# Gate and up products of the shared FFN in two fp16 parts

## The chip, the cores and the metric

The kernel is one program on one core of a Trainium2 chip. The metric is the device time of an execution in microseconds (us). It computes an adaLN transformer block: attention with 16 heads over two sequences of 2048 tokens of width 256, then a feed-forward part (FFN) made of a shared expert that sees every token and eight routed experts, one for each token.

## The reference, cut to what matters

```python
h = layernorm(x) * (1 + ca) + sa
x = x + ga * attention(h)                      # 16 heads of 16, LoRA folded into the weights
h = layernorm(x) * (1 + cb) + sb               # called h2 in the kernel
logits = h @ gate_w.T                          # 4096 x 8
top_id, score = argmax(logits), sigmoid(max(logits))
shared = (silu(h @ shared_gate.T) * (h @ shared_up.T)) @ shared_down.T     # F = 512
routed = swiglu of expert top_id on h * score
x = x + gb * (shared + routed)
```

All of it is in f32 at the outside; 4096 tokens, width D = 256 (two halves of 128), F = 512 (four blocks of 128).

## The kernel before, in words

Tokens go in eight chunks of 512. The kernel has no scheduler: every engine has a stream written out by hand, and semaphores join them.

**Heads** (attend_tensor, attend_vector, attend_scalar, attend_gpsimd, attend_sync). For each of 32 heads TensorE makes score products twice: once for the row maxima, into a ring of three PSUM banks that VectorE reduces (L1374; one in eight is folded in with ScalarE's help, L1416, L1371), and once for the exponentials, which ScalarE takes (L1437) and TensorE multiplies with the values (L1305). The maxima are made one to two heads ahead. These score products are in fp16 parts already (L1237, L1293). ScalarE copies the finished head out of PSUM (L1443). SP's stream has a list of transfers by head, in `prepare(n)`: with head 9 it loads `wuT` and `wdT`, the shared FFN's weights. GpSimd's stream has elementwise work of other stages by head (bias of the residual rows with heads 4 and 7, for example), each time ahead of `split_maxima`, whose `mb` the head's scores need. In head 20 VectorE inverts the first sums in eight pieces (L1071).

**Merge** (merge_tensor, merge_vector, merge_scalar, merge_sync). For each chunk: output projection (L1652), residual (L1721) and moments on VectorE, root (L1757), VectorE's factors, normalisation on ScalarE (L1764, `normalize2`), transposes on TensorE into banks 2 and 3 (`turn`), and `take` on ScalarE (L1772), which copies the two banks out as `h2T` in f32 with the modulation's scale and shift. Then logits (`route_logits`, `turn_logits`, `take_turned_logits`, `take_logits`). ScalarE's order in turn g is take(g - 2), root2(g), take_turned_logits(g - 3), take_logits(g - 4), normalize2(g). The four blocks of the shared FFN's first chunk are woven in at the end. SP stores the rows; when the last are stored (`merged`) it issues 17 loads of 512 KB with the routed experts' weights: one `rgT`, eight `ruT`, eight `rdT`. `wgT` is loaded at the start of this stage.

**Shared FFN** (shared_tensor, shared_scalar, shared_vector, shared_sync, scatter_gpsimd). For chunk g and block fc TensorE makes gate and up (L1622, `gate_up`) into a pair of banks; two pairs alternate, so TensorE is at most two blocks ahead of VectorE. ScalarE takes SiLU of the gate (L1981), VectorE multiplies with up (L1825). After the four blocks of chunk g + 1 TensorE makes the down product of chunk g (L1959). VectorE's stream is residual(g), then the four products of chunk g + 2: residual(g) is a multiplication (L1996) and an addition of the residual rows `xr` (L2000), which SP has loaded. Beside it GpSimd works through 32 tiles of 128 tokens: multiply (L1929), copy of tags, add (L1936), and an indirect DMA to the sorted place (L1942), with four buffers `sc_x`. SP loads those rows, and its stream has in this order: rows of tiles 0 to 3, `xr` of chunks 0 and 1, tiles 4 to 7, and then for g = 0, 1, 2: tiles of set 2g + 2, store of chunk g, `xr` of chunk g + 2, tiles of set 2g + 3. Each load of token rows waits for its buffer's last scatter, each `xr` for the store of its buffer. After that come store 3, `xr` of chunk 5, a wait for all scatters, and the first sorted tiles.

The routing (route_vector, L1836 to L1878) ranks the tokens by expert on VectorE; the first scatter waits for it.

**Routed experts**: 39 tiles of 128 sorted rows, gate and up (L2086) and down (L2109).

## Time and profile before

| | us |
|---|---|
| three runs | 1747.12, 1747.13, 1748.29 |
| their median | 1747.13 |
| the profiled execution | 1743.12 |
| its span, first to last instruction | 1741.1 |

Three runs of one program lie 1.2 us apart; the profiled execution is 4.0 us under the median. In the profile PE is TensorE's matmuls and PEld its weight loads, DVE is VectorE, ACT ScalarE, POOL GpSimd, SP the queue engine. In a timeline row stand the start in us, the length in us, the engine, the line, the operation with its tiles (out<-in), how many neighbours of one kind were merged in it, and in brackets how long the engine had been idle and what ended that. A merged row's length covers all of it. A granted clock of 1.00 is TensorE's full 2.4 GHz.

### The profile page before, as it was taken

Reading aid. Unit: us, or ns where it says so; the run is one execution under the profiler, and the core shown is the slowest. Engines: PE = TensorE matmul, PEld = TensorE weight load, DVE = VectorE, ACT = ScalarE, POOL = GpSimd, SP = SyncE. Lnnn points to the kernel's source line nnn. Section 1 sums busy time; section 2 is a strip of 40 time slices with the busy share of each in tenths; the row PEclk is TensorE's granted clock in tenths of the full one; section 3 lists DMA queues with packets and bytes.
Section 4 is the critical chain, followed back from the end, with each engine's and each line's share of the span. In section 5 each row is a group of like instructions: output and inputs, shape, how many; then the busy total and the mean of one; then the engine's idle time right before and its main releaser. Section 6 shows DMA issues by size and latency. Waiting matters only on the chain.

```text
span 1741.1 us, 31097 instructions
## 1 busy us (share of the span) xinstructions
PE 1681.1 (97%) x11097; PEld 650.6 (37%) x11098; DVE 1374.7 (79%) x2723; ACT 1332.6 (77%) x1662; POOL 333.1 (19%) x427
## 2 busy tenths in 40 slices
PE   9999999999999999999999999999989999999997
PEld 5532222222222222222222222222217555799996
DVE  7689999999999999999999999999906422355553
ACT  5449999999999999999999999999997211244442
POOL 5525020040000000000001000001010377133332
PEclk9999999999999999999999999999999999999998
DMA  7322021131110111101322001131025633322221
GB/s 234 99 66 74 30 80 34 70 93 42 43 58 22 31 52 34 34 22 34 92 61 55 22 31 33 48 88 38 27 78 217 266 107 122 118 74 67 66 69 39
DMA packets 76509, 124.93 MB, mean 72 GB/s; under 512 B 15652, under 2 KB 49141, under 8 KB 76252
## 3 DMA queue, kind: packets, MB, share of 16 engines
q1 hardware_dynamic: 67628, 99.33, 18.3%
q0 software_dynamic: 7792, 22.57, 3.9%
q8 instruction: 77, 1.26, 0.3%
q10 hardware_dynamic: 960, 1.34, 0.3%
q14 instruction: 52, 0.43, 0.1%
HBM read 76.50 MB, written 47.21 MB: 71 GB/s over the span
## 4 chain that ended last, share of the span: by engine, by line
PE 82%; DVE 10%; ACT 5%; issue 3%; DMA 0%; POOLq 0%; POOL 0%; ACTq 0%; DVEq 0%
PE ps L1305 27%; PE ps L1237 18%; DVE mx L1374 8%; PE ps L2086 8%; PE ps L1293 8%; PE ps L1622 6%; PE ps L2109 4%; ACT prob L1437 4%; PE ps L1959 3%; PE ps L780 3%; PE ps L1652 2%; PE ps L799 2%; ACT step_sb L1416 1%; PE ps L2065 0%; PE ps L1266 0%
## 5 line engine op out<-in xcount | busy, mean ns | idle before, releaser
L1437 ACT ACTIVATE prob<-ps 128x1024 f32<-128x1024 f32 x1024 | 1000.8, 1049 | 75.0 <-PE ps L1293 74.8
L1374 DVE TENSOR_REDUCE mx<-ps 128x1 f32<-128x512 f32 x1558 | 1000.7, 685 | 64.0 <-PE ps L1237 43.4
L1237 PE MATMUL ps<-k_high,q_high 48*128 48x512 f16 x1803 | 545.5, 383 | 24.3 <-DVE mx L1374 0.2
L1305 PE MATMUL ps<-prob,vs 128*32 128x512 f32 x4096 | 545.5, 605 | 4.3 <-ACT prob L1437 3.5
L1293 PE MATMUL ps<-q_high,k_high 50*128 50x512 f16 x2048 | 419.0, 382 | 1.6 <-ACT prob L1437 1.6
L1237 PEld LDWEIGHTS ps<-k_high,q_high 48*128 48x128 f16 x1803 | 128.9, 93 | 596.6 <-DVE mx L1374 413.4
L1371 DVE CUSTOM_DVE_ANT_0 step_sb<-ps,step_sb 128x512 f32<-128x512 f32 x245 | 166.8, 681 | 0.0
L1293 PEld LDWEIGHTS ps<-q_high,k_high 50*128 50x128 f16 x2048 | 100.4, 94 | 168.5 <-ACT prob L1437 161.3
L1466 POOL CAST mb<-turned_sb 16x128 f16<-16x128 f32 x32 | 9.0, 280 | 768.6 <-ACT turned_sb L1423 755.1
L1416 ACT ACTIVATE step_sb<-ps 128x512 f32<-128x512 f32 x245 | 150.6, 615 | 0.2 <-PE ps L1237 0.2
L1305 PEld LDWEIGHTS ps<-prob,vs 128*32 128x32 f32 x4096 | 80.6, 107 | 167.5 <-issue 140.1
L1981 ACT ACTIVATE sgate<-ps 128x512 f32<-128x512 f32 x32 | 19.1, 597 | 117.4 <-PE ps L1622 117.4
L2135 ACT ACTIVATE esig<-ps 128x512 f32<-128x512 f32 x39 | 23.3, 597 | 111.4 <-PE ps L2086 111.4
L2169 DVE TENSOR_TENSOR ehT<-esig,ps 128x512 f32<-128x512 f32 x39 | 26.8, 688 | 98.9 <-PE ps L2086 98.9
L1237 PE MATMUL ps<-k_step,q_high 48*128 48x512 f16 x245 | 94.7, 386 | 0.0
L1825 DVE TENSOR_TENSOR hid<-sgate,ps 128x512 f32<-128x512 f32 x32 | 22.0, 688 | 72.5 <-ACT sgate L1981 72.1
L2086 PEld LDWEIGHTS ps<-xsT,gate_w 128*128 128x128 f32 x624 | 75.6, 192 | 1.9
L2086 PE MATMUL ps<-xsT,up_w 128*128 128x128 f32 x624 | 76.0, 275 | 0.0
L2086 PE MATMUL ps<-xsT,gate_w 128*128 128x128 f32 x624 | 76.0, 275 | 0.0
L2109 PE MATMUL ps<-rdT,ehT 128*128 x312 | 73.6, 379 | 0.0
L2086 PEld LDWEIGHTS ps<-xsT,up_w 128*128 128x128 f32 x624 | 72.8, 192 | 0.0
L2229 POOL DMA_INDIRECT x_in<-x_rows,cix x39 | 37.7, 967 | 153.0 <-DVE eout L2196 110.0
(195 smaller groups left out, 1407.7 us busy)
## 6 DMA issues: line engine op xcount, KB each, us to landing
qk_parts<-parts SPq DMA_DIRECT2D x32, 256.0 KB, 2.4
k_high<-qk_parts SPq DMA_DIRECT2D x63, 128.0 KB, 2.7
head_out<-head_out_sb SPq DMA_DIRECT2D x31, 256.0 KB, 2.5
sorted_in<-zero_row POOLq DMA_DIRECT2D x13, 390.0 KB, 3.7
xs<-sorted_in SPq DMA_DIRECT2D x39, 130.0 KB
xg<-in_x SPq DMA_DIRECT2D x8, 512.0 KB, 5.4
...
```

The costliest lines, as they stand in the source:

```text
L780: mm = pe.matmul(ps[:, 2 + n % 2, :], wqkv[:, o // 2, k, (o % 2) * P:(o % 2 + 1) * P], hT[g % CPB][:, k, :], start=(k == 0), stop=(k == 1))
L1237: pe.matmul(ps[:, ring.bank((n, m, u)), :], q_high[p][mine, t * P:(t + 1) * P], keys, start=True, stop=True).then_inc(s_max, 1)
L1293: mm = pe.matmul(ps[:, bank + u, :], k_high[p][mine, kt * P:(kt + 1) * P], q_high[p][mine, i * CH:(i + 1) * CH], start=True, stop=True)
L1305: mm = pe.matmul(ps[32 * j:32 * j + 32, 7, :], vs[buf(h)][:, kt, :], prob[:, (kt + 1) % 2, j * CH:(j + 1) * CH], start=(kt == 0), stop=(kt ...
L1371: dve.tensor_tensor_reduce(step_sb[:], bank, step_sb[:], 1.0, LOWEST, ALU.add, ALU.max, largest).then_inc(s_ring, 1)
L1374: dve.tensor_reduce(largest, bank, AX.X, ALU.max).then_inc(s_ring, 1)
L1416: act.activation(step_sb[:], bank, ACT.Relu).then_inc(s_turned, 1)
L1437: act.activation(prob[:, (kt + 1) % 2, :].rearrange("p (u c n) -> p u c n", u=2, c=2)[:, :, half, :], ps[:, bank:bank + 2, :], ACT.Exp, sc ...
L1622: mm = pe.matmul(ps[:, at, :], w[:, k, fc * P:(fc + 1) * P], h2T[:, k, bass.ds(g * CH, CH)], start=(k == 0), stop=(k == 1))
L1959: mm = pe.matmul(ps[:, DOWN_BANK[u] + t // 2, t % 2 * D:(t % 2 + 1) * D], hid[u][:, fc, t * P:(t + 1) * P], wdT[:, fc, :], start=(fc == 0) ...
L2086: mm = pe.matmul(ps[:, bank, fc * P:(fc + 1) * P], w[u][:, c, fc * P:(fc + 1) * P], xsT[u][:, c, :], start=(c == 0), stop=(c == 1))
L2109: mm = pe.matmul(ps[:, 6 + u, 0:D], ehT[u][:, c, :], rdT[:, bass.ds(e, 1), c, :].squeeze(1), start=(c == 0), stop=(c == FC - 1))
```

## The change

The rows `h2` and the weights of gate and up are each held as two fp16 tiles, a high part and the difference to it, after scaling by powers of two so that both parts fit fp16's range. Each f32 product becomes three fp16 products: high by high, high weight by low row, low weight by high row.

- Both raw weights and `wdT` are loaded with head 9. In head 12 VectorE takes the largest absolute value of each partition (`largest_value`, two tensors of 1024 elements, one of 8); SP stores them and with head 14 loads all of them back to each partition; in head 17 VectorE makes scales and factors in nine small operations (`ffn_units`). In heads 18 and 19 GpSimd scales the modulation's columns and splits the weights (`split_weights`).
- In `take` ScalarE copies the two banks twice: as f32 into `h2T`, which has two buffers now and feeds the logits, and as fp16 into the high part. GpSimd subtracts (`split_rows`, one operation over 1024 elements a chunk) in front of its scatter stream. The transposes of the next chunk wait for the second pair of copies.
- `h2T`'s buffers lie where the last two experts' `rdT` will be. So their two loads move from the end of merge_sync to shared_sync, behind token_rows(1), with waits for all logits and all differences.
- The factor that undoes the scaling rides on SiLU (a register), on VectorE's product (scalar_tensor_tensor in place of tensor_tensor) and on the copy of the logits.
- `wgT`'s load at the start of the merge goes.

The diff, without constants, semaphores and the layout of buffers:

```diff
...
@@ -324,10 +337,11 @@
         l_in = buffers("l_in", [P, HALF, CH], F32, r, CPB)
         o_in = buffers("o_in", [P, HALF, CH], F32, r, CPB)
         xg = buffers("xg", [P, TPC, D], F32, Region(nc, down_at, queries_at), CPB)
+        h2T = buffers("h2T", [P, HALF, CH], F32, Region(nc, top - 2 * 4 * FC * D, top))
         o_first = buffers("o_first", [P, HALF, CH], F32, Region(nc, stage_at, stage_at + 4 * KT * D), CPB)
 
         r = Region(nc, stage_at, late_at)
-        h2T = r("h2T", [P, HALF, T])
+        h2_parts = r("h2_parts", [P, NCH, 2, HALF, CH], F16)
         after_h2T = r.at
 
         xg += [r(f"xg{g}", [P, TPC, D]) for g in range(CPB, NCH)]
...
@@ -1159,8 +1175,15 @@
                         store_key_steps(sp, 1, half)
                 if n == XB_AT + 5:
                     sp.wait_ge(s_kstepst, 16 * HALF * B)
-                    for dst, name in ((wuT, "wuT"), (wdT, "wdT")):
+                    for dst, name in ((raw_gate, "wgT"), (raw_up, "wuT"), (wdT, "wdT")):
                         sp.dma_start(dst[:], io[name]).then_inc(s_shared, 16)
+                if n == TOPS_AT + 1:
+                    sp.wait_ge(s_range, 10)
+                    sp.dma_start(tops_dram, tops[:]).then_inc(s_shared, 16)
+                if n == TOPS_AT + 2:
+                    sp.wait_ge(s_shared, 64)
+                    sp.dma_start(all_tops[:].rearrange("p q v -> p (q v)"),
+                                 tops_dram.rearrange("q v -> (q v)").partition_broadcast(P)).then_inc(s_shared, 16)
                 if n == XB_AT + 1:
                     sp.wait_ge(s_xgst, 16 * CPB)
                     for c in range(CPB):
...
@@ -1381,12 +1404,44 @@
                 dve.wait_ge(s_neg, n + 1)
                 dve.memset(mx[n][:, 0:HT, STEP:STEP + 1], LOWEST)
 
+        TOP_TURNS = (8, 14, 20)
+
+        def largest_value(dve, i):
+
+            if i == 0:
+                dve.wait_ge(s_shared, 48)
+            if i == 2:
+                dve.wait_ge(s_colffn, 16 * 4 * B)
+            source = (raw_gate[:].rearrange("p k f -> p (k f)"), raw_up[:].rearrange("p k f -> p (k f)"),
+                      colffn[:].rearrange("p b v k -> p (b v k)"))[i]
+            dve.tensor_reduce(tops[:, i:i + 1], source, AX.X, ALU.max, apply_absolute_value=True).then_inc(s_range, 1)
+
+        def ffn_units(dve, step):
+
+            dve.wait_ge(s_shared, 80)
+            step(dve.tensor_reduce(largest[:], all_tops[:].rearrange("p q v -> p v q"), AX.X, ALU.max))
+            step(dve.tensor_scalar(largest[:], largest[:], TINY, None, ALU.max))
+            step(dve.tensor_scalar(ffn_scale[:].bitcast(U32), largest[:].bitcast(U32), EXPONENT, EXPONENT,
+                                   ALU.bitwise_and, ALU.bitwise_xor))
+            step(dve.tensor_scalar(top_power[:].bitcast(U32), largest[:].bitcast(U32), EXPONENT, None, ALU.bitwise_and))
+            step(dve.tensor_scalar(ffn_scale[:, 0:2], ffn_scale[:, 0:2], WEIGHT_UNIT / 2, None, ALU.mult))
+            step(dve.tensor_scalar(ffn_scale[:, 2:3], ffn_scale[:, 2:3], ROW_UNIT / 2, None, ALU.mult))
+            for i in range(2):
+                step(dve.scalar_tensor_tensor(ffn_restore[:, i:i + 1], top_power[:, i:i + 1],
+                                              1.0 / (WEIGHT_UNIT * ROW_UNIT), top_power[:, 2:3], ALU.mult, ALU.mult))
+            dve.tensor_scalar(ffn_restore[:, 2:3], top_power[:, 2:3], 1.0 / ROW_UNIT, None,
+                              ALU.mult).then_inc(s_range, 1)
+
         def attend_vector(dve, step):
             for n in range(1, NH):
                 for m in range(BESIDE if n == 1 else 0, PAIRS):
                     reduce_pair(dve, (0, n), m)
                     if m == 1:
                         negate(dve, n - 1)
+                    if n == TOPS_AT and m in TOP_TURNS:
+                        largest_value(dve, TOP_TURNS.index(m))
+                    if n == TOPS_AT + 5 and m == TOP_TURNS[0]:
+                        ffn_units(dve, step)
                     if n == FIRST_AT + 3 and m % 4 == 0:
                         invert(dve, 0, m // 4)
                     if n == NEXT_AT + 3 and m % 8 == 0:
...
@@ -1465,6 +1520,14 @@
             pool.wait_ge(s_mrows[p], 64 + MROWS * (n // NB))
             step(pool.tensor_copy(mb[p][:, 0, :], turned_sb[:]))
             pool.tensor_tensor(mb[p][:, 1, :], turned_sb[:], mb[p][:, 0, :], ALU.subtract).then_inc(s_mb, 1)
+
+        def split_weights(pool, step, raw, w_parts, i):
+
+            flat = raw[:].rearrange("p k f -> p (k f)")
+            high, low = (w_parts[:, part].rearrange("p k f -> p (k f)") for part in range(2))
+            step(pool.tensor_tensor(flat, flat, ffn_scale[:, i:i + 1].to_broadcast([P, HALF * F]), ALU.mult))
+            step(pool.tensor_copy(high, flat))
+            pool.tensor_tensor(low, flat, high, ALU.subtract).then_inc(s_range, 1)
 
         def attend_gpsimd(pool, step):
             pool.wait_ge(s_late, 16 * len(late_loads))
...
@@ -1525,6 +1588,14 @@
                     bias(1, 0)
                     for half in range(HALF):
                         key_steps(pool, step, half)
+                if n == TOPS_AT + 6:
+                    pool.wait_ge(s_range, 11)
+                    pool.tensor_tensor(colffn[:].rearrange("p b v k -> p (b v k)"),
+                                       colffn[:].rearrange("p b v k -> p (b v k)"),
+                                       ffn_scale[:, 2:3].to_broadcast([P, 2 * B * HALF]), ALU.mult).then_inc(s_range, 1)
+                    split_weights(pool, step, raw_gate, wg_parts, 0)
+                if n == TOPS_AT + 7:
+                    split_weights(pool, step, raw_up, wu_parts, 1)
                 if n == FIRST_AT + 6:
                     pool.wait_ge(s_oin, 16 * 4 * CPB)
                     for c in range(CPB):
...
@@ -1598,7 +1668,7 @@
             sp.dma_start(rgT[:, E - 1:E], io["rgT"][:, E - 1:E]).then_inc(s_expert_late, 16)
             for e in range(E):
                 sp.dma_start(ruT[:, e:e + 1], io["ruT"][:, e:e + 1]).then_inc(s_expert_late, 16)
-            for e in range(E):
+            for e in range(E - 2):
                 sp.dma_start(rdT[:, e:e + 1], io["rdT"][:, e:e + 1]).then_inc(s_expert_late, 16)
 
         def merged(eng):
...
@@ -1615,12 +1685,14 @@
 
             bank = GATE_BANK[fc % 2]
             pe.wait_ge(s_gu_free, FC * g + fc + 1)
-            for w, at in ((wgT, bank), (wuT, bank + 1)):
+            for w, at in ((wg_parts, bank), (wu_parts, bank + 1)):
                 if between and at > bank:
                     between()
                 for k in range(HALF):
-                    mm = pe.matmul(ps[:, at, :], w[:, k, fc * P:(fc + 1) * P],
-                                   h2T[:, k, bass.ds(g * CH, CH)], start=(k == 0), stop=(k == 1))
+                    for wp, hp in ((0, 0), (0, 1), (1, 0)):
+                        mm = pe.matmul(ps[:, at, :], w[:, wp, k, fc * P:(fc + 1) * P],
+                                       h2_parts[:, bass.ds(g, 1), hp, k, :].squeeze(1), start=(k == 0 and hp + wp == 0),
+                                       stop=(k == 1 and wp == 1))
             mm.then_inc(s_gu, 1)
 
         def route_ranks(pe):
...
@@ -1767,17 +1839,23 @@
 
             def take(g):
                 act.wait_ge(s_n2T, g + 1)
+                wait(act, s_h2_parts, g - 1)
+                wait(act, s_lgp, g - 1)
                 b = g // CPB
                 for k in range(HALF):
-                    a = act.activation(h2T[:, k, g * CH:(g + 1) * CH], ps[:, 2 + k, :], ACT.Identity,
+                    a = act.activation(h2T[g % 2][:, k, :], ps[:, 2 + k, :], ACT.Identity,
                                        bias=colffn[:, b, 0, k:k + 1], scale=colffn[:, b, 1, k:k + 1])
                 a.then_inc(s_h2T, 1)
+                for k in range(HALF):
+                    a = act.activation(h2_parts[:, g, 0, k, :], ps[:, 2 + k, :], ACT.Identity,
+                                       bias=colffn[:, b, 0, k:k + 1], scale=colffn[:, b, 1, k:k + 1])
+                a.then_inc(s_h2_high, 1)
 
             def take_logits(g):
                 act.wait_ge(s_lgx, g + 1)
-                act.copy(logits[:, TPC * g:TPC * (g + 1), :],
-                         ps[:, LOGIT_BANK[g > CPB], 0:P].rearrange("p (t e) -> p t e", e=32)[:, :, 0:E]
-                         ).then_inc(s_lg, 1)
+                act.activation(logits[:, TPC * g:TPC * (g + 1), :],
+                               ps[:, LOGIT_BANK[g > CPB], 0:P].rearrange("p (t e) -> p t e", e=32)[:, :, 0:E],
+                               ACT.Identity, scale=ffn_restore[:, 2:3]).then_inc(s_lg, 1)
 
             def take_turned_logits(g):
                 act.wait_ge(s_lgp, g + 1)
...
@@ -1902,6 +1981,10 @@
             load(0)
             load(1)
             token_rows(1)
+            sp.wait_ge(s_lgp, NCH)
+            sp.wait_ge(s_h2_parts, NCH)
+            for e in range(E - 2, E):
+                sp.dma_start(rdT[:, e:e + 1], io["rdT"][:, e:e + 1]).then_inc(s_expert_late, 16)
             for g in range(3):
                 token_rows(2 * g + 2)
                 store(g)
...
@@ -1920,6 +2003,14 @@
             store(6)
             store(7)
 
+        def split_rows(pool, step):
+
+            for g in range(NCH):
+                high, low = (h2_parts[:, g, part].rearrange("p k t -> p (k t)") for part in range(2))
+                flat = h2T[g % 2][:].rearrange("p k t -> p (k t)")
+                pool.wait_ge(s_h2_high, g + 1)
+                pool.tensor_tensor(low, flat, high, ALU.subtract).then_inc(s_h2_parts, 1)
+
         def scatter_gpsimd(pool, step):
             pool.wait_ge(s_zero, 16 * (NTILE // ZERO + 1))
 
...
@@ -1965,6 +2056,8 @@
                 for fc in range(FC):
                     gate_up(pe, g, fc)
 
+            pe.wait_ge(s_shared, 48)
+            pe.wait_ge(s_h2_parts, NCH)
             with pe.Fori(0, NCH // 2 - 1) as i:
                 for u in range(2):
                     gate_up_all(2 * i + u + 1)
...
@@ -1975,16 +2068,17 @@
             turn_in(pe, (0, 0))
             down(NCH - 1, 1)
 
-        def shared_silu(act, g, fc):
+        def shared_silu(act, g, fc, gate_scale):
             act.wait_ge(s_gu, FC * g + fc + 1)
             act.wait_ge(s_gu_free, FC * g + fc + 1)
-            act.activation(sgate[fc % 2][:], ps[:, GATE_BANK[fc % 2], :], ACT.Silu).then_inc(s_silu, 1)
-
-        def shared_scalar(act):
+            act.activation(sgate[fc % 2][:], ps[:, GATE_BANK[fc % 2], :], ACT.Silu, scale=gate_scale
+                           ).then_inc(s_silu, 1)
+
+        def shared_scalar(act, gate_scale):
             route_scalar(act)
             with act.Fori(1, NCH) as g:
                 for fc in range(FC):
-                    shared_silu(act, g, fc)
+                    shared_silu(act, g, fc, gate_scale)
 
         def shared_vector(dve, step):
             def hidden(g, u):
```

## Rows read from the trace of the kernel before

**Rows 1.** The page: busy time of each engine, share of the span.

```profile
PE 1681.1 (97%) x11097; PEld 650.6 (37%) x11098; DVE 1374.7 (79%) x2723; ACT 1332.6 (77%) x1662; POOL 333.1 (19%) x427
```

**Rows 2.** Timeline of ScalarE, copies of a finished head: start us, us.

```profile
759.76 0.63 ACT L1443 COPY head_out_sb<-ps 128x512 f32<-128x512 f32 x1
...
796.75 0.63 ACT L1443 COPY head_out_sb<-ps 128x512 f32<-128x512 f32 x1
...
833.93 0.63 ACT L1443 COPY head_out_sb<-ps 128x512 f32<-128x512 f32 x1
```

**Rows 3.** Stretches: from:to, length, busy of PE, PEld, DVE, ACT, POOL; clock, DMA.

```profile
240.00:280.00 40.00, 38.68 (x281) 8.51 (x282) 38.18 (x72) 37.59 (x47) 12.07 (x10) 1.00 0.34 98
...
1320.00:1340.00 20.00, 20.00 (x158) 16.60 (x157) 15.84 (x50) 16.67 (x38) 0.00 (x0) 1.00 0.77 298
...
1560.00:1580.00 20.00, 20.00 (x152) 19.17 (x151) 11.40 (x32) 9.10 (x11) 6.28 (x7) 1.00 0.21 60
...
1732.00:1734.00 2.00, 0.00 (x0) 0.00 (x0) 0.00 (x0) 0.00 (x0) 0.00 (x0) 0.59 0.02 0
```

**Rows 4.** Timeline of TensorE, the shared FFN's start and end.

```profile
1362.29 1.88 PE L1622 MATMUL ps<-h2T,wgT 128*128 x4
...
1496.43 1.88 PE L1622 MATMUL ps<-h2T,wgT 128*128 128x512 f32 x4
...
1498.14 1.88 PE L1622 MATMUL ps<-h2T,wuT 128*128 128x512 f32 x4
...
1499.86 7.07 PE L1959 MATMUL ps<-wdT,hid 128*128 128x256 f32 x32
...
1514.11 1.95 PE L2086 MATMUL ps<-xsT,gate_w 128*128 128x128 f32 x16
```

**Rows 5.** Timeline of VectorE, residual and products behind the fifth xr load.

```profile
1469.15 1.23 DVE L2000 TENSOR_TENSOR xr<-xr,ymod 128x1024 f32<-128x1024 f32 x1 [2.05 <-DMA xr<-x_rows]
...
1470.57 0.69 DVE L1825 TENSOR_TENSOR hid<-sgate,ps 128x512 f32<-128x512 f32 x1 [0.20 <-DVE xr L2000]
```

**Rows 6.** Timeline of TensorE in the heads, fp16 products.

```profile
701.46 0.38 PE L1293 MATMUL ps<-q_high,k_high 50*128 50x512 f16 x2
...
701.68 0.38 PE L1237 MATMUL ps<-k_high,q_high 48*128 48x512 f16 x1
```

**Rows 7.** ScalarE's groups: busy us, mean ns of one, idle before.

```profile
L877 ACT ACTIVATE parts<-ps,bqk,unit_scale 128x512 f16<-128x512 f32 x32 | 24.6, 770 | 0.0
...
L1772 ACT ACTIVATE h2T<-ps,colffn 128x512 f32<-128x512 f32 x16 | 11.5, 768 | 1.6 <-PE ps L1661 1.5
```

**Rows 8.** Timeline of SP's queue: issues.

```profile
1346.19 0.32 SPq L1578 DMA_DIRECT2D n_rows<-n  x1
...
1348.93 0.33 SPq L1598 DMA_DIRECT2D rgT<-in_rgT  x1
...
1465.26 0.32 SPq L1888 DMA_DIRECT2D xr<-x_rows  x1
...
1480.83 0.32 SPq L1888 DMA_DIRECT2D xr<-x_rows  x1
```

**Rows 9.** GpSimd's groups in the heads.

```profile
L963 POOL TENSOR_TENSOR step_parts<-k_from,step_parts 128x512 f16<-128x512 f32 x2 | 2.3, 1160 | 0.2
```

**Rows 10.** Timeline of GpSimd, the first token rows.

```profile
1374.72 1.41 POOL L1929 TENSOR_TENSOR sc_x<-sc_x,rowmod 128x256 f32<-128x256 f32 x2 [84.97 <-DMA sc_x<-n_rows]
...
1378.62 1.09 POOL L1942 DMA_INDIRECT sorted_in<-sc_x,slot  x1 [0.17 <-issue]
```

**Rows 11.** Timeline of VectorE, the last step of the routing.

```profile
1373.14 0.18 DVE L1878 TENSOR_SCALAR tile_e<-tile_f 128x39 uint32<-128x39 f32 x1
```

**Rows 12.** VectorE's groups in the first 200 us.

```profile
L673 DVE TENSOR_REDUCE largest_w<-wqkv 128x4 f32<-128x1024 f32 x1 | 1.2, 1220 | 0.0
```

**Rows 13.** Line 1071 by itself: duration ns min/median/max, starts.

```profile
L1071 DVE RECIPROCAL sums<-sums x13: 341/343/940, 822.3 to 1265.3; 128x32 f32<-128x32 f32 x12, 96x128 f32<-96x128 f32 x1
```

**Rows 14.** The page's costliest groups: weight loads of fp16 products.

```profile
L1237 PEld LDWEIGHTS ps<-k_high,q_high 48*128 48x128 f16 x1803 | 128.9, 93 | 596.6 <-DVE mx L1374 413.4
```

57 lines of the change are left out of this document (37 added, 20 removed).

## The prediction

> **What bounds the kernel now.** First the page's busy line [rows 1]: TensorE is busy for 97% of the span. That is an average over four stages, so I read stage by stage and asked which wait ends last in each.
>
> The attention heads. Their period is the distance of two copies of a head's result: 36.99 us, with one of 37.18 [rows 2]. Over 40 us TensorE, VectorE and ScalarE are busy for 38.68, 38.18 and 37.59 [rows 3]; all three are nearly full and hand each other work through three PSUM banks.
>
> The second normalisation (1308 to 1362 us). TensorE is full and ScalarE busy 16.67 of 20 us [rows 3]: ScalarE is close behind.
>
> The shared FFN (1362 to 1514 us). The profile splits each fp32 product in two records. A group of four, which is one weight's two products for one block of F, takes 1498.14 - 1496.43 = 1.71 us, so gate and up of a block 3.43; a down product takes 6.9, from (1514.11 - 1499.86)/2 less a transpose [rows 4]. TensorE is full here, but two chains beside it have their own pace: GpSimd's scatter of the sorted rows, and SP's queue, which feeds the scatter and loads the residual rows `xr` in between, in program order. VectorE waited for one `xr` load already: 2.05 us, until 1469.15 [rows 5]. That wait is hidden today because TensorE has two blocks of lead.
>
> The routed experts. TensorE 20.00 of 20 us [rows 3]; this stage moves as a whole with its start, 1514.11.
>
> So the question is how much earlier or later the routed stage starts, plus what the heads lose.
>
> **The change, part by part.**
>
> 1. *Fewer passes.* Each fp32 product becomes three fp16 products. No fp16 product over all 128 rows stands in the trace; the nearest are those of the heads, which follow each other at 701.46, 701.68: 0.22 us [rows 6] (two of half height share one such slot). I take 0.215, hence 12 x 0.215 = 2.58 us for a block instead of 3.43. Over 32 blocks that is 27 us of TensorE's time. Bounds: 0.11 (two half-height products in a slot) and 0.38 (one product's own duration). The Trainium skill (TensorE: Matmul & The Clock Gate, Back-to-back issue gap) gives for a stream of weight loads and products a roofline of about 131 ns at 512 columns; the row does not bear it out, and by it a block would take an estimated 1.57 us. I price it as a rival.
>
> 2. *ScalarE in the normalisation.* Each of 8 chunks gets two more copies out of PSUM. The present two take 11.5/16 = 0.72 us each, and one with fp16 output 770 ns, as with f32 [rows 7]. So +1.44 us a chunk. Six such chunks stand on ScalarE ahead of the last normalised chunk: at most 8.6 us. ScalarE's idle time, 3.3 us in 20 [rows 3], is mostly short waits for VectorE's factors that stay; I take 2 us of cover and put the last normalised rows 6.6 us later. They are stored at 1346.19, and behind that store SP queues the expert loads at 1348.93 [rows 8]. GpSimd's differences (fp16 out, 512 elements: 1160 ns [rows 9], so 2.3 us a chunk) fit in the 5 us and more that a chunk takes (20 us full of TensorE hold four [rows 3]): nothing.
>
> 3. *Expert loads.* 17 loads of 512 KB go ahead of the first token rows: from 1348.93 to their arrival, seen as GpSimd's first `scale` at 1374.72 [rows 8, 10], 25.8 us or 1.5 each. Two (`rdT` of the last two experts) move behind the second set of token rows: the first rows come 3.0 us sooner against the queue's start. Together 6.6 - 3.0 = 3.6 us later, and the first scatter with it (1378.62 to 1382.2). Routing must be done by then. The last logits wait for two more long copies, so routing ends about 8 us later, 1373.3 + 8 = 1381.3 [rows 11]: just covered, by 0.9 us; if the cover goes, the scatter starts later by what is missing. The two moved loads then sit in front of token rows in the DMA queues: 0 to 3.0 us, I take 0.8, since only the rows issued right behind them meet them. New waits of SP (all logits, all differences) have ended long before. Sum: the scatter chain, and with it every `xr` load, is 4.4 us late. The scatter's own pace doesn't change: it is a loop of load, add, scatter and landing over four buffers, and TensorE isn't in it.
>
> 4. *The shared stage by the new chain.* TensorE began chunk 1 at 1362.29 and would now begin near 1370 (8 us later, as routing). It would then run five chunks of 10.3, five downs of 6.9 and two blocks, 91 us, with some 3 us of small waits, and stand at 1465 before block 2 of chunk 6. That block needs VectorE's products of the same chunk, behind residual 4, which needs the fifth `xr` load: 1469.15 + 4.4 = 1473.6. TensorE stalls for about 11 us. From the load's arrival on: 2.1 us to VectorE's next product (1470.57 + 0.69 - 1469.15 [rows 5]), two blocks 5.2, down 6.9, chunk 7's four blocks 10.3, and 14.25 from the last block to the first routed product [rows 4]: 38.7. Against the old times 1469.15 + 38.7 = 1507.9, which is 6.3 before 1514.11; with the delay of 4.4 only 1.9 is left. The next `xr` load is issued 15.6 us behind (1465.26, 1480.83 [rows 8]) and is not late.
>
> 5. *The clock.* At the kernel's end, with TensorE idle, the granted clock of 1732 to 1734 is 0.59 of full [rows 3], between the upper level and the lower one, 1.2 GHz. I take it that after a stall of 11 us TensorE restarts at the lower one. No row shows when it returns: bounds 0 and the whole of the two blocks at half speed, +5.2. I take +2.0, between them.
>
> 6. *Heads.* VectorE gets two reductions over 1024 elements (1220 ns [rows 12]), a small one, and in one head a chain of nine small operations, some 2.1 us. Nearest row: eight reciprocals of 0.34 us, 2.7 us in all, spread over a head, cost 37.18 - 36.99 = 0.2 [rows 2, 13]. Bursts as long as two or three reductions empty the three banks, so more is lost: between 0.4 and the full 4.7 us; I take 2.0. GpSimd's scaling, cast and difference of the two weights run where it had 12 us of work in 40 without harm [rows 3]: nothing. If that cover went, it would be `mb` of head 18 or 19 late.
>
> 7. *Nothing else.* The factor in SiLU, in VectorE's product and in the logits' copy ride on instructions that exist; the register load lies in ScalarE's wait before the first root. The load of `wgT` leaves a busy queue of 0.5 MB: nothing.
>
> Sum: -1.9 + 2.0 + 2.0 = +2.1 us. The profiled execution took 1743.12 (span 1741.1), 4.0 below the median of 1747.13; on the median the forecast is **1749.2 us**, +0.12%. About 0.2% (3.5 us) is what a measurement here can tell from no change. The change saves 27 us of TensorE's work and TensorE waits instead.
>
> **Rivals.**
> - *TensorE keeps the pace.* If the fifth `xr` load came by 1462 instead of 1473.6, nothing would bind and the stage would end 12 us early: 1737. For: this is what a TensorE at 97% suggests. Against: [rows 5], the load is late already in the slower kernel. 0.07.
> - *Half of the loss doesn't come*: ScalarE's idle time covers more, heads lose 0.5, the clock is back at once. the scatter is 2.5 late: -6.3 + 2.5 + 0.5 = -3.3, 1743.8. 0.10.
> - *The bursts in the heads cost what they last* (slower). Place: heads 12 and 17 on VectorE; price 4.7 us instead of 2; it decides as soon as the three banks hold less than one burst. With the rest as forecast +4.8: 1752. For: VectorE is busy 38.18 of 40. Against: the head with 2.7 us more lost 0.2. 0.20.
> - *The clock stays low* for the two blocks, or the moved loads or late routing hold the scatter by the upper bound: +3 more, 1752.5. 0.12.
> - *The skill's roofline*: six blocks behind the load are 1.0 shorter each, -6: 1743. The page is the one named under 1. 0.03.
> - *It doesn't do what it says*: fp16 weight loads not hidden, 93 ns [rows 14] on each of 72 products behind the load, +7: 1756. 0.03.
>
> **How the numbers follow.** Forecast 0.45, its own range 1746 to 1751. Range with the neighbours on both sides: 1742 to 1754. Slower by over 0.2%: 0.20 + 0.12 + 0.03 = 0.35, of which some stay below 3.5 us, while the forecast's own spread passes it about as often: 0.34. Faster: 0.07, with most of the next case and the roofline, 0.17. Same: 0.49.
>
> **What would show it.** Groups of TensorE's blocks 2.58 us apart; two more ScalarE copies a chunk and the last normalised store about 6.6 us later relative to the last head; the first scatter 3 to 5 us later; VectorE waiting some 12 us for `xr` in chunk 4 and TensorE idle there for 11 with the granted clock at half behind it; heads 12 and 17 longer by a microsecond each. If TensorE has no idle stretch between 1450 and 1480, the forecast is wrong, and likewise if the heads lose over 3 us.

## The result, and the profile after

| | before | after |
|---|---|---|
| median of the runs, us | 1747.12 (5 runs, 1745.46 to 1748.29) | 1758.47 (5 runs, 1755.83 to 1761.45) |
| profiled execution | 1743.12 | 1757.7 |
| its span | 1741.1 | 1755.9 |

The ratio is 1.0073, 95% interval 1.0062 to 1.0084: slower by 11 to 15 us. The forecast was 1749.2 with a range up to 1754, so it was too low, and the range missed it.

The medians differ by 11.4 us. The profiled spans, of which alone the account below is made, differ by 14.8 us: the profiled execution of the kernel before lies 4.0 us under the median of its first three runs, that of the kernel after 0.8 under its own. The page says that TensorE has less to do and the kernel is longer:

```profile
PE 1665.8 (95%) x11225; PEld 640.6 (36%) x11226; DVE 1390.1 (79%) x2735; ACT 1344.7 (77%) x1678; POOL 360.8 (21%) x442
```

Against [rows 1], TensorE is busy 15.3 us less, ScalarE 12.1 and VectorE 15.4 more. Where the 14.8 us come from is read in four places.

**The heads.** ScalarE's copies of finished heads, in the kernel before and then in the kernel after. Heads are counted by these copies, from 0; VectorE works a head ahead, so what stands under heads 12 and 17 in the diff falls into heads 11 and 16 here. Head 11 (with both reductions of VectorE) took 576.61 - 538.03 = 38.58 and head 16 took 40.25 instead of 36.98. The last head's copy is at 1310.14; before it was at 1305.12. That is +5.0.

```profile
1305.12 0.58 ACT L1443 COPY head_out_sb<-ps 128x512 f32<-128x512 f32 x1 [1.41 <-PE ps L1305]
```

```profile
538.03 0.63 ACT L1498 COPY head_out_sb<-ps 128x512 f32<-128x512 f32 x1
576.61 0.63 ACT L1498 COPY head_out_sb<-ps 128x512 f32<-128x512 f32 x1
...
724.54 0.63 ACT L1498 COPY head_out_sb<-ps 128x512 f32<-128x512 f32 x1
764.79 0.63 ACT L1498 COPY head_out_sb<-ps 128x512 f32<-128x512 f32 x1
...
1310.14 0.58 ACT L1498 COPY head_out_sb<-ps 128x512 f32<-128x512 f32 x1 [1.41 <-PE ps L1328]
```

The insertions on VectorE's timeline: two reductions of 1.21 us, and nine small operations that last from 722.81 to 725.22.

```profile
536.30 1.21 DVE L1417 TENSOR_REDUCE tops<-raw_gate 128x1 f32<-128x1024 f32 x1
543.53 1.21 DVE L1417 TENSOR_REDUCE tops<-raw_up 128x1 f32<-128x1024 f32 x1
...
722.81 0.69 DVE L1422 TENSOR_REDUCE largest<-all_tops 128x3 f32<-128x384 f32 x1
...
725.07 0.15 DVE L1432 TENSOR_SCALAR ffn_restore<-top_power 128x1 f32<-128x1 f32 x1
```

In head 16 more was lost than the 2.4 us of the chain. TensorE's timeline and the stretches of 2 us behind it (the figure behind POOL's busy time is the granted clock):

```profile
725.88 0.39 PE L1260 MATMUL ps<-k_high,q_high 48*128 48x512 f16 x1 [1.54 <-DVE mx L1397]
```

```profile
726.00:728.00 2.00, 2.00 (x11) 0.40 (x12) 2.00 (x5) 1.41 (x2) 0.00 (x0) 0.84 0.91 287
728.00:730.00 2.00, 2.00 (x12) 0.29 (x6) 0.91 (x3) 0.58 (x2) 0.00 (x0) 0.50 0.46 161
730.00:732.00 2.00, 2.00 (x15) 0.41 (x11) 1.84 (x5) 2.00 (x3) 0.00 (x0) 0.80 0.02 5
```

TensorE had been idle for 1.54 us, waiting for VectorE, and ran for some us at half clock afterwards; VectorE, which had the long list, now waits for TensorE (busy 0.91 of 2). The lost clock is 2 x (0.16 + 0.50 + 0.20) = 1.7 us of TensorE's time.

**The second normalisation.** Each of the last four chunks takes 7.0 us (ScalarE's normalisations start 1339.59, 1346.59) instead of about 5. ScalarE, VectorE and GpSimd in one such chunk:

```profile
1339.59 2.08 ACT L1836 ACTIVATE n<-xg,shift,std 128x256 f32<-128x256 f32 x4 [1.74 <-DVE shift L1810]
...
1346.59 2.08 ACT L1836 ACTIVATE n<-xg,shift,std 128x256 f32<-128x256 f32 x4 [1.74 <-DVE shift L1810]
```

```profile
1337.76 1.79 DVE L1810 SCALAR_TENSOR_TENSOR shift<-mv,std 128x4 f32<-128x4 f32 x1
```

```profile
1337.41 2.13 POOL L2012 TENSOR_TENSOR h_parts<-h2T,h_parts 128x1024 f16<-128x1024 f32 x1 [5.81 <-ACT h_parts L1850]
```

VectorE's `shift`, four numbers in each partition, takes 1.79 us; before the change it took 0.16:

```profile
1338.69 0.16 DVE L1738 SCALAR_TENSOR_TENSOR shift<-mv,std 128x4 f32<-128x4 f32 x1
```

It ends when GpSimd's difference ends (1337.41 + 2.13 = 1339.54), and ScalarE stands still for 1.74 us waiting for it. This is so in the last four of the eight chunks, where GpSimd begins when ScalarE has finished the high part, which is just when ScalarE's root releases VectorE's factors. In the first four chunks `shift` takes 0.16 us; in two of these GpSimd's difference meets another two-input operation of VectorE instead, the product `o_in`, which takes 1.88 and 2.40 us for 0.69 before the change. The later of the two, with the free `shift` behind it:

```profile
1329.75 2.40 DVE L1787 TENSOR_TENSOR o_in<-o_in,l_in 32x512 f32<-32x512 f32 x1
...
1332.39 0.16 DVE L1810 SCALAR_TENSOR_TENSOR shift<-mv,std 128x4 f32<-128x4 f32 x1
```

The Trainium skill (SBUF — State Buffer, Who interferes with whom) says of the port pair that VectorE and GpSimd share that it is "an exclusive lock"; an operation of VectorE with two SBUF inputs against one of GpSimd is its case, and the rows of VectorE and GpSimd above agree with it.

Behind the stage, the queue of SP, GpSimd's first token rows and the end of the routing:

```profile
1362.67 0.32 SPq L1649 DMA_DIRECT2D n_rows<-n  x1
1365.42 0.33 SPq L1668 DMA_DIRECT2D rgT<-in_rgT  x1
```

```profile
1388.70 1.59 POOL L2020 TENSOR_TENSOR sc_x<-sc_x,rowmod 128x256 f32<-128x256 f32 x2 [13.56 <-DMA sc_x<-n_rows]
...
1393.02 1.09 POOL L2033 DMA_INDIRECT sorted_in<-sc_x,slot  x1 [0.17 <-issue]
```

```profile
1391.31 0.76 DVE L1957 TENSOR_SCALAR tile_e<-tile_f 128x39 uint32<-128x39 f32 x1
```

Against [rows 8, 10], last store and expert loads are 16.5 us later, the first scatter 14.4: 5.0 of that from the heads, 9.4 from this stage.

**The shared FFN.** VectorE waits twice for `xr`, TensorE twice for VectorE:

```profile
1457.78 1.22 DVE L2094 TENSOR_TENSOR xr<-xr,ymod 128x1024 f32<-128x1024 f32 x1 [5.79 <-DMA xr<-x_rows]
...
1486.26 1.23 DVE L2094 TENSOR_TENSOR xr<-xr,ymod 128x1024 f32<-128x1024 f32 x1 [10.85 <-DMA xr<-x_rows]
```

```profile
1460.01 1.58 PE L1693 MATMUL ps<-h_parts,wg_parts 128*128 x6 [4.11 <-DVE hid L1904]
...
1488.49 2.74 PE L1693 MATMUL ps<-h_parts,wg_parts 128*128 x6 [9.36 <-DVE hid L1904]
...
1526.90 1.95 PE L2180 MATMUL ps<-xsT,gate_w 128*128 128x128 f32 x16
```

The fifth `xr` load lands 17.1 us later than in [rows 5], the routed stage starts 12.8 later than in [rows 4]. From the first scatter to that landing it is 93.24 us, before 1469.15 - 1378.62 = 90.53: 2.7 more.

**The routed experts** take 1.9 us more from their start to TensorE's last down product.

So 5.0 (heads) + 9.4 (merge) + 2.7 (from first scatter to fifth `xr`) - 4.3 (from there to the routed stage: 40.64 for 44.96) + 1.9 = 14.7 of 14.8.

### The profile page after: what moved, and what is told of

Read it like the earlier page. It is cut to its first block, busy times and chain, and to the rows that moved or that the text cites. A ratio compares the mean times of both kernels' runs of the same rounds, so it can differ in the third digit from the quotient of the medians.

```text
span 1755.9 us, 31418 instructions
## 1 busy us (share of the span) xinstructions
PE 1665.8 (95%) x11225; PEld 640.6 (36%) x11226; DVE 1390.1 (79%) x2735; ACT 1344.7 (77%) x1678; POOL 360.8 (21%) x442
## 4 chain that ended last, share of the span: by engine, by line
PE 73%; DVE 10%; ACT 5%; DMA 5%; issue 4%; POOL 2%; SPq 1%; POOLq 0%; ACTq 0%; DVEq 0%
PE ps L1328 27%; PE ps L1260 18%; PE ps L2180 8%; DVE mx L1397 8%; PE ps L1316 8%; PE ps L2203 4%; ACT prob L1492 3%; PE ps L796 3%; DMA sc_x<-n_rows 2%; DMA sorted_in<-sc_x,slot 2%; PE ps L815 2%; PE ps L2050 1%; PE ps L1693 1%; POOL sc_x L2020 1%; ACT step_sb L1471 1%
## 5 line engine op out<-in xcount | busy, mean ns | idle before, releaser
L796 PE MATMUL ps<-hT,wqkv 128*128 128x512 f32 x128 | 65.3, 617 | 0.0
```

The lines of the kernel that those rows point to most:

```text
L796: mm = pe.matmul(ps[:, 2 + n % 2, :], wqkv[:, o // 2, k, (o % 2) * P:(o % 2 + 1) * P], hT[g % CPB][:, k, :], start=(k == 0), stop=(k == 1))
```

## The experiments

The theory after the result: TensorE's saved time is worth nothing while the scatter and `xr` chain sets the pace, and that chain is moved back by three things, each visible above: bursts on VectorE in the heads, `shift` held by GpSimd, and the `rdT` loads in front of token rows. The table puts all runs on one scale. The columns are times of the profiled execution: the copy of the last head, and from there to SP's first expert load, to the first scatter and to the first routed product; then the span and the ratio to the kernel before in the same session. The kernel before had medians of 1743.3 to 1747.1 us in the five sessions, so spans from different sessions compare only to some 4 us; the ratios are free of that. The columns of times are one execution each, and that of e8 was the slowest of its eleven.

| | last head | expert loads | first scatter | routed stage | span | ratio, 95% interval |
|---|---|---|---|---|---|---|
| before | 1305.12 | 43.81 | 73.50 | 208.99 | 1741.1 | |
| after | 1310.14 | 55.28 | 82.88 | 216.76 | 1755.9 | 1.0073 (1.0062 to 1.0084) |
| e1 spread | 1307.55 | 55.28 | 82.69 | 217.49 | 1755.3 | 1.0064 (1.0047 to 1.0080) |
| e2 clear | 1311.49 | 48.16 | 75.92 | 209.50 | 1751.9 | 1.0035 (1.0022 to 1.0047) |
| e3 xr on ScalarE | 1309.82 | 55.27 | 82.80 | 213.58 | 1753.7 | 1.0059 (1.0042 to 1.0076) |
| e4 the same, in before | 1305.08 | 43.78 | 73.40 | 208.96 | 1744.4 | 1.0002 (0.9992 to 1.0012) |
| e5 high part on GpSimd | 1309.82 | 44.03 | 70.98 | 208.30 | 1745.1 | 1.0014 (1.0004 to 1.0023) |
| e6 rdT later | 1311.43 | 55.26 | 83.03 | 214.56 | 1753.0 | 1.0056 (1.0041 to 1.0072) |
| e7 one product | 1308.52 | 55.27 | 82.70 | 211.89 | 1747.4 | 1.0038 (1.0023 to 1.0053) |
| e8 all, first try | 1323.61 | 43.80 | 71.08 | 198.82 | 1751.6 | 1.0017 (1.0008 to 1.0027) |
| e9 all, SP's queue | 1311.49 | 43.78 | 71.16 | 189.99 | 1734.5 | 0.9943 (0.9927 to 0.9960) |
| e10 all, ScalarE's queue | 1311.82 | 43.78 | 70.95 | 198.60 | 1741.6 | 0.9981 (0.9970 to 0.9991) |
| e11 e9, turn ahead | 1312.52 | 43.80 | 70.86 | 196.93 | 1740.1 | 0.9981 (0.9971 to 0.9990) |
| e12 e9, units later | 1306.24 | 43.77 | 70.97 | 189.63 | 1725.5 | 0.9899 (0.9883 to 0.9916) |

**e1: VectorE's insertions in pieces.** The reductions over 1024 elements become four each, and one piece or one small operation stands at a time between two pairs:

```diff
-                    if n == TOPS_AT and m in TOP_TURNS:
-                        largest_value(dve, TOP_TURNS.index(m))
-                    if n == TOPS_AT + 5 and m == TOP_TURNS[0]:
-                        ffn_units(dve, step)
+                    if n == TOPS_AT and m >= 3 and m % 3 == 0 and m <= 24:
+                        largest_piece(dve, step, (m // 3 - 1) // 4, (m // 3 - 1) % 4)
...
+                    if n == TOPS_AT + 5 and 4 <= m <= 24 and m % 2 == 0:
+                        ffn_unit(dve, step, (m - 4) // 2)
...
```

> VectorE's reductions and small operations of heads 12 and 17 in pieces of 0.4 us and less, each three turns or two apart. Theory (a burst longer than what the three banks hold stalls TensorE for its rest): the two heads that took 38.58 and 40.25 us take at most 37.3 each, the last head ends 4.2 us or more sooner, and the time falls by that, 4 us. Rival (VectorE has no slack, added work costs what it lasts, however it is cut): both heads keep 1.4 and 3 us more and the time stays within 1 us of the changed kernel.

The last head came at 1307.55: 2.4 us over before instead of 5.0. So 2.6 us were won, not the 4.2 of the theory, and nearly all of it in one of the two places. The chain of small operations cost 3.3 us as a burst and costs 0.9 in pieces (heads 15 and 16 took 37.24 and 37.59); 1.3 of the gain is the low clock, which doesn't come here. The reductions cost 1.6 us as two bursts and 1.6 as eight pieces of 0.41 us, 3.3 us in all (heads 10 and 11 took 37.27 and 38.26): there the rival, added work costs whatever its form, fits better. The ratio moved by 0.0009, which its interval doesn't tell from nothing; the 2.6 us are read from the heads.

**e2: GpSimd keeps clear of `shift`.** One line; the difference of chunk g waits until VectorE has made the factors of chunk g + 2:

```diff
+                pool.wait_ge(s_shift2, min(g + 3, NCH))
```

> GpSimd's difference of a chunk waits until VectorE's shift factors of the chunk two further on are made; nothing else. Theory (the shift's scalar_tensor_tensor, which reads two SBUF tiles, is held while GpSimd's difference runs, 1.79 us instead of 0.16): it takes 0.2 us again, the distance of two normalised chunks falls from 7.0 to about 5.4 us, the expert loads start some 7 us sooner, and the routed stage starts 6 to 8 us sooner. Rival (the operation is slow for another reason, or the period is set by ScalarE's longer copies alone): the period stays over 6.5 us and the time changes by less than 2.

VectorE's `shift`, GpSimd's difference and ScalarE's normalisation of this kernel:

```profile
1338.49 0.16 DVE L1810 SCALAR_TENSOR_TENSOR shift<-mv,std 128x4 f32<-128x4 f32 x1
```

```profile
1338.80 2.15 POOL L2013 TENSOR_TENSOR h_parts<-h2T,h_parts 128x1024 f16<-128x1024 f32 x1 [3.22 <-DVE shift L1810]
```

```profile
1338.69 2.08 ACT L1836 ACTIVATE n<-xg,shift,std 128x256 f32<-128x256 f32 x4
1344.06 2.08 ACT L1836 ACTIVATE n<-xg,shift,std 128x256 f32<-128x256 f32 x4
```

`shift` is 0.16 us again, a chunk takes 5.37, and the expert loads go 7.1 us sooner behind the last head. The same two operations of the same size, only moved apart, so the held instruction was the cause and not ScalarE's copies. Those copies, a fourth cause beside the three named above, cost what is left: 48.16 - 43.81 = 4.4. (e5 takes them away, and nearly all of it goes.)

**e3 and e4: `xr` off SP's queue.** Stores and loads of `xr` for chunks 2 to 7 go on ScalarE's queue, behind its SiLU:

```diff
...
+                if g >= 2:
+                    act.wait_ge(s_x2, g)
+                    act.dma_start(rows(x2_dram, (g - 2) * TPC, TPC), xr[g % 2][:]).then_inc(s_x2st[g % 2], 16)
+                    act.wait_ge(s_x2st[g % 2], 16 * (g // 2))
+                    act.dma_start(xr[g % 2][:], x1_dram[g]).then_inc(s_xr[g % 2], 16)
```

> The stores and loads of the residual rows of chunks 2 to 7 are issued from ScalarE's queue, behind its work of the chunk, in place of SP's. Theory (TensorE waits for VectorE, which waits for xr, whose load stands behind token rows in SP's stream): no stall of TensorE between 1455 and 1490, no half clock, the shared stage at TensorE's pace: routed stage at about 1509.5 instead of 1526.9, time 17 us less than the changed kernel. Rival (the scatter of token rows binds as hard): the routed stage starts no sooner than 1520.

> The same move in the kernel before. Theory (there TensorE's own work sets the pace of the shared stage and the late xr load is covered): VectorE's wait of 2.05 us goes and the time stays within 1 us. Rival (SP's queue bound the stage in the kernel before too): 3 us or more faster.

In e3 no wait for `xr` is left, but the routed stage comes only 3.2 us sooner behind the last head, at 1523.40, as the rival had it: TensorE then waits 10.86 us for the first sorted tiles, so the scatter chain binds next. It has also become longer itself: from the first to the last scatter of token rows 115.3 us, 109.0 in the kernel after (more of this at e10). TensorE's timeline and SP's load of the first sorted tiles:

```profile
1513.07 0.66 PE L2155 MATMUL ps<-ident,xs 128*128 128x128 f32 x2 [10.86 <-DVE xs L2161]
...
1523.40 1.95 PE L2176 MATMUL ps<-xsT,gate_w 128*128 128x128 f32 x16
```

```profile
1510.45 1.76 SPq L2140 DMA_DIRECT2D xs<-sorted_in  x4
```

e4 makes the same move in the kernel before: ratio 1.0002, routed stage at 1514.04 against 1514.11. VectorE's 2.05 us wait for `xr` is gone, and nothing is won. There TensorE set the pace (from 1370 to 1530 the kernel before has no idle time of TensorE above 0.6 us), and the place of `xr` in SP's queue cost nothing.

**e5: GpSimd makes the high part too.** ScalarE goes back to two copies a chunk; GpSimd casts `h2T` and subtracts, both behind `shift`:

```diff
...
-                for k in range(HALF):
-                    a = act.activation(h2_parts[:, g, 0, k, :], ps[:, 2 + k, :], ACT.Identity,
-                                       bias=colffn[:, b, 0, k:k + 1], scale=colffn[:, b, 1, k:k + 1])
-                a.then_inc(s_h2_high, 1)
...
-                pool.wait_ge(s_h2_high, g + 1)
+                pool.wait_ge(s_h2T, g + 1)
+                pool.wait_ge(s_shift2, min(g + 3, NCH))
+                step(pool.tensor_copy(high, flat))
```

> ScalarE's take is as in the kernel before (two copies); GpSimd makes the high part from h2T, then the difference, both only after VectorE's shift factors of the chunk two further on. Theory (ScalarE's two more copies and the held shift factors stretch the normalisation from 5.2 to 7.0 us a chunk and delay everything behind it by 11 us): a chunk takes 5.2 to 5.6 us, the last normalised rows are stored 42 us behind the last head's copy (52.5 in the changed kernel, 41.1 before), and the routed stage starts 9 us sooner than in the changed kernel. Rival (GpSimd's 3.2 us a chunk now hold VectorE or the logits as much): over 6.3 us a chunk and less than 4 us gained.

```profile
1343.91 1.04 POOL L2009 CAST h_parts<-h2T 128x1024 f16<-128x1024 f32 x1 [1.56 <-DVE shift L1810]
1345.03 2.15 POOL L2010 TENSOR_TENSOR h_parts<-h2T,h_parts 128x1024 f16<-128x1024 f32 x1
```

GpSimd needs 3.2 us in a chunk of 5.2, between two `shift`s, and the expert loads are at 44.03 behind the last head: as before the change. The first scatter is 2.5 us earlier than before; 15 loads stand ahead of it and not 17. This one repair takes back most of the loss: 1.0014.

**e6: the last two `rdT` behind the last token rows.** The waits and the two loads move, as they are, behind the loop that loads token rows.

> The loads of rdT for the last two experts stand behind the last token rows and the last xr of the loop in SP's stream. Theory (in front of the third set of token rows they cost the scatter chain 1.4 to 2.7 us, which go through to the end): the fifth xr load lands 1.4 to 2.7 us sooner relative to the first scatter, time 1.4 to 2.7 us less than the changed kernel. Rival (they are hidden in the chain's own waits): no change within 0.5 us in the trace.

From the first scatter (1394.46) to the fifth `xr` (1484.28) it takes 89.8 us, 93.2 with the loads where the change had put them. So they cost 3.4 us there, all that two loads take (3.0 by the forecast's 1.5 each). The routed stage behind the last head gains 2.2. The ratio, 1.0056, has an interval that overlaps that of the kernel after, so these figures too are the trace's alone.

The heads of this kernel tell something else. Its head 16 took 41.82 us, with VectorE's stream the same as in the kernel after. Over all kernels with the nine operations in one burst, that head's length goes with the clock of the stretch behind it. Stretches of e6, then one of e5, whose head 16 took 38.96:

```profile
728.00:730.00 2.00, 2.00 (x11) 0.42 (x7) 1.24 (x2) 0.95 (x3) 0.00 (x0) 0.50 0.34 124
730.00:732.00 2.00, 2.00 (x13) 0.30 (x10) 1.88 (x4) 1.72 (x2) 0.00 (x0) 0.50 0.02 5
732.00:734.00 2.00, 2.00 (x11) 0.43 (x7) 0.65 (x3) 0.14 (x1) 0.00 (x0) 0.50 0.00 0
```

```profile
728.00:730.00 2.00, 2.00 (x16) 0.47 (x16) 2.00 (x4) 1.67 (x3) 0.00 (x0) 1.00 0.91 347
```

| kernel | clock lost in 726 to 736, us | head 16, us |
|---|---|---|
| e5, e7 | 0 | 38.96, 38.96 |
| after, e2, e3 | 1.7 each | 40.25, 40.29, 40.29 |
| e6 | 3.4 | 41.82 |

(Clock lost is 2 us times one less the granted clock, summed over the five stretches.) So the burst itself costs 38.96 - 36.98 = 2.0 us, and the low clock that may follow costs 0, 1.3 or 2.9 more.

**e7: one product instead of three.**

```diff
-                    for wp, hp in ((0, 0), (0, 1), (1, 0)):
+                    for wp, hp in ((0, 0),):
```

> Only the high by high product is made; the two with a low part are left out, a block takes 0.86 us instead of 2.59. Theory (TensorE waits for the xr chain and only its work behind the last late load counts): 48 us of TensorE's work go between the first block and the routed stage, and the stage starts only about 7 us sooner, with longer stalls. Rival (TensorE's products set the pace): 30 us or more sooner.

```profile
1457.80 1.03 PE L1693 MATMUL ps<-h_parts,wg_parts 128*128 x2 [16.80 <-DVE hid L1904]
...
1487.13 1.04 PE L1693 MATMUL ps<-h_parts,wg_parts 128*128 x2 [16.41 <-DVE hid L1904]
```

Two thirds of the products gone, 8 in each of 28 blocks at 0.216 = 48 us of TensorE's work in this stage, and the routed stage comes 6.5 us sooner, 1.6 of it from the heads. The rest became idle time, 16.8 and 16.4 us at these two places instead of 4.1 and 9.4, shorter waits elsewhere, and time at a low clock (0.50 from 1450 to 1460 and from 1480 to 1490). TensorE isn't what limits this stage after the change.

**e8: all repairs at once.** Insertions over two heads each, e5, e6, e3, and the turn of the first sorted tiles behind the last down product (VectorE's residual of chunk 6 goes ahead of its scaling of those tiles with it):

```diff
...
-            turn_in(pe, (0, 0))
             down(NCH - 1, 1)
+            turn_in(pe, (0, 0))
```

> All together: VectorE's work of the heads in pieces over two heads each, GpSimd makes both parts, the two rdT loads late, xr on ScalarE's queue, and the first sorted tile's transposes behind the last down product. Theory (the three fp16 products are worth 27 us once nothing else is late; what is left is the scatter chain at 3.6 us a tile from about 1376 on): the routed stage starts at 1495 to 1499 instead of 1514 in the kernel before, time 15 to 19 us less than it, ratio 0.989 to 0.992. Rival (the scatter of token rows starts or runs later with TensorE, GpSimd and the transfers all denser): 1505 or later, ratio above 0.995.

A miss: ratio 1.0017. The profiled execution is the slowest of eleven, 7.0 us over their median of 1746.74, so the sizes that follow are those of its worst case. Behind the heads it is 10 us ahead of before, but the heads lost 18.5, since the insertions had been moved ahead of the transfers that feed them. VectorE's timeline:

```profile
501.83 0.42 DVE L1413 TENSOR_REDUCE pieces<-raw_gate 128x1 f32<-128x256 f32 x1 [7.16 <-DMA wdT<-in_wdT]
...
695.19 0.32 DVE L1430 TENSOR_REDUCE largest<-all_tops 128x1 f32<-128x128 f32 x1 [3.94 <-DMA all_tops<-largest_values]
```

The wait of 7.16 made head 9 last 47.03, 10.0 too long, and the wait of 3.94 made head 14 last 43.64, 6.7 too long.

**e9, e10, e11: the same repairs, placed later.** The pieces stand in two heads each at TOPS_AT, + 1, + 5 and + 6, with SP's transfers and GpSimd's split one head later than in the change. e10 keeps `xr` on ScalarE's queue. e9 and e11 keep it on SP's in another order, and e11 leaves the turn (and VectorE's residual) where the change had it. The two `rdT` loads stand behind the loop in all three:

```diff
...
-            for g in range(3):
-                token_rows(2 * g + 2)
-                store(g)
-                load(g + 2)
-                token_rows(2 * g + 3)
-            store(3)
-            load(5)
+            for g in range(6):
+                token_rows(g + 2)
+                store(g)
+                load(g + 2)
```

> All repairs together, transfers left on SP's queue but in an order in which token rows and xr alternate: VectorE's insertions spread over four heads with the loads that feed them placed one head later, GpSimd making both high part and difference after the shift op, the two rdT rows behind the last token rows, the turn of the first sorted tiles behind the last shared down product. Theory (heads' surplus, held shift op, xr chain are the whole loss): last head copy within 1.5 us of the kernel before's 1305.1, first scatter near 1376, no xr stall over 3 us, and the routed stage starts at 1500 to 1506 because the scatter chain (117 us from first scatter to xs, less its waits) now sets it; 1738 to 1742 us, ratio 0.994 to 0.997. Rival (something else in the change costs): routed stage not before 1512, ratio 1.000 or over.

> As the run beside it, but xr's stores and loads on ScalarE's queue and SP's order as it was. Theory: the same heads; no xr wait at all; routed stage at 1500 to 1504, ratio 0.993 to 0.996. Rival (ScalarE's waits for the stores hold its activations and so TensorE, as they could in the last chunks): stalls of TensorE over 3 us before the last chunk, routed stage 1508 or later.

> As the first of the three, but the turn of the first sorted tiles ahead of the last shared down product, as in the kernel changed. If the scatter chain sets the start, TensorE waits there for xs and the routed stage starts 2 to 4 us later than in the first; if TensorE sets it, both are within 1 us.

e9 beats both kernels, 0.9943. No wait for `xr` is left, and the routed stage starts 19 us sooner behind the last head than before. Only the heads fall short: 1311.49 and not 1306.6. e10's routed stage is as late as its rival had it, but not for the rival's reason: from 1375 to 1495 TensorE has no idle time above 0.6 us, and then it waits 11.65 us for the first sorted tiles. What is late is the scatter chain. From the first to the last scatter of token rows it takes 120.3 us, in e9 110.6, although nothing stands between the token rows in e10's SP stream. GpSimd's longest waits for token rows, 4.1 and 4.3 us, come right behind a store and a load of `xr` on ScalarE's queue:

```profile
1434.10 0.33 ACTq L2096 DMA_DIRECT2D xr<-x_rows  x1
```

```profile
1438.83 0.72 POOL L2030 TENSOR_TENSOR sc_x<-sc_x,rowmod 128x256 f32<-128x256 f32 x1 [4.12 <-DMA sc_x<-n_rows]
```

The other kernels with that move have a longer chain too: e3 115.3 for the 109.0 of the kernel after, e4 110.3 for the 106.1 of the kernel before, e8 120.3. It takes the wait for `xr` away and lengthens the scatter chain; by what path wasn't tried. With it e10 loses 8.6 us behind the last head. e11 starts its routed stage 8.0 us behind e9 (6.9 counted from the last head), more than the 2 to 4 expected: TensorE waits 8.86 us for `xs` with a down product of 7.1 queued behind the wait, which e9 does in that time.

In e9 the head that ends at 728.95 took 42.15 us. VectorE's row and a stretch of TensorE behind it:

```profile
721.35 0.32 DVE L1430 TENSOR_REDUCE largest<-all_tops 128x1 f32<-128x128 f32 x1 [3.80 <-DMA all_tops<-largest_values]
```

```profile
724.00:726.00 2.00, 2.00 (x10) 0.20 (x8) 1.40 (x3) 1.16 (x2) 0.00 (x0) 0.50 0.10 32
```

**e12: e9 with the scale factors and the split one head later.**

```diff
...
-                    if n in (TOPS_AT + 5, TOPS_AT + 6) and m % 5 == 4:
-                        ffn_unit(dve, step, m // 5 + 6 * (n - TOPS_AT - 5))
+                    if n in (TOPS_AT + 6, TOPS_AT + 7) and m % 5 == 4:
+                        ffn_unit(dve, step, m // 5 + 6 * (n - TOPS_AT - 6))
...
```

> The best kernel so far, with VectorE's scale factors (the small operations behind the load of all partitions' largest values) and GpSimd's split one head later; the head in which VectorE waited 3.80 us for that load was 5.2 us too long. Theory (only that wait costs there): that head back within 0.5 us of 36.99, last head copy at 1306 to 1307.5, routed stage at 1496 to 1498, 1731 to 1733 us, ratio 0.991 to 0.9935. Rival (the routed stage's start is set by the scatter chain, not by what is ahead of it): the last head copy comes as early, but the routed stage gains less than 2 us.

```profile
723.74 0.63 ACT L1519 COPY head_out_sb<-ps 128x512 f32<-128x512 f32 x1
760.78 0.61 ACT L1519 COPY head_out_sb<-ps 128x512 f32<-128x512 f32 x1
```

```profile
1494.00 0.44 PE L2171 MATMUL ps<-ident,xs 128*128 128x128 f32 x2 [2.94 <-DVE xs L2177]
...
1495.87 3.62 PE L2192 MATMUL ps<-xsT,gate_w 128*128 128x128 f32 x16
```

1725.77 us, ratio 0.9899, lower than expected. The wait and its low clock are gone (the last head is at 1306.24), and the routed stage starts 5.6 us sooner than in e9. The routed stage itself is 3.4 us shorter than e9's, which neither theory had; in e9 TensorE waits 21 times for VectorE's turned tiles there (7.4 us in all), in the kernel after 9 times (3.2 us), in e12 and before never. What sets that off wasn't tried. The eight pieces of the reductions, spread over more heads, cost 0.9 us in e12 and not 1.6 as in e1, the small operations 0.2.

In the profiled executions e12 is 15.6 us under the kernel before: 19.4 won between the last head and the routed stage, 1.1 lost in the heads and 2.6 behind the routed stage's start. All of the change's arithmetic is kept, both products of low parts too; what made it slow was where its side work stood, and on which engine. One comparison is missing: SP's new order and the later turn were not put into the kernel before. They take waits away, and that kernel's TensorE has none above 0.6 us in this stage, so they should be worth little there, but no run shows it.

## Why the prediction was wrong, step by step

- **Step 1, fewer passes: right.** TensorE's six products of one weight follow each other 1383.99 - 1382.70 = 1.29 us apart (rows below), so a block takes 2.59 for the 2.58 forecast, and its weight loads are hidden. The roofline rival didn't come.

```profile
1382.70 1.46 PE L1693 MATMUL ps<-h_parts,wg_parts 128*128 x6
1383.99 1.46 PE L1693 MATMUL ps<-h_parts,wu_parts 128*128 x6
```

- **Step 2, the normalisation: wrong, and the largest error.** "GpSimd's differences ... nothing" was argued from their length alone, 2.3 us in 5. What they hold was not asked. They held `shift` and with it ScalarE, 1.6 us in each of the last four chunks, and an `o_in` product in two earlier ones. The expert loads were 11.5 us late behind the heads instead of 6.6; without that hold (e2) they are 4.4 late, so the 6.6 put down for ScalarE's copies was itself 2.2 too much.
- **Step 3, expert loads: wrong through step 2 and by a term of its own.** First scatter +9.4 and not +3.6; the routing's last step came 18.2 later than in [rows 11] and ended 1.0 ahead of the first scatter (1392.07, 1393.02), covered as narrowly as forecast. The two moved loads were put at 0.8 between 0 and 3.0; the traces say 2.7, and e6 says 3.4. The reason given ("only the rows issued right behind them meet them") doesn't hold: the whole length of the loads went through to the fifth `xr`, which fits with those rows being one turn of the loop that everything behind waits for.
- **Step 4, the shared stage by the new chain: right.** The binding wait is the fifth `xr`, as named. From its landing to the routed stage it took 40.64, forecast 38.7 + 2.0 for the clock. TensorE's stall was 9.4 for 11. An earlier stall of 4.1 at chunk 5 was not foreseen; it hides behind the later one.
- **Step 5, the clock: right in size.** The first block behind the stall took 4.30 us (1488.49 to 1492.79) for 2.59, its first half 2.54 for 1.29, so 1.7 was lost for the 2.0 forecast; from 1492 on the granted clock was 1.00 again.
- **Step 6, heads: wrong.** 2.0 was taken between 0.4 and 4.7; 5.0 was measured. The rival "cost what they last" has nearly the total but not its make-up: 1.6 in head 11 for two reductions of 1.2 each, 2.0 in head 16 for the chain of 2.4, and 1.3 by the low clock behind the second. That a VectorE burst drops TensorE's clock was in no part of the prediction.
- **Step 7, nothing else: wrong by 1.9**, in the routed stage.

Sum of the errors: heads 3.0, merge 9.4 - 3.6 = 5.8, loads 2.7 - 0.8 = 1.9, routed stage 1.9, together 12.6. The forecast's +2.1 and these make 14.7, the 14.8 of the profiled spans (11.4 by the medians). The three named unknowns were each taken below the middle of their bounds, and the one with the largest error had no bounds at all.

The forecast that TensorE's gain of 27 us becomes idle time was right (e7), and it explains why the kernel isn't faster; it doesn't explain why it is slower. That is the side work: e5 alone brings 1.0073 to 1.0014, and all repairs give 0.9899.
